# First loads, constants and key masks of a two-layer decoder kernel rearranged

## The chip, the cores and the metric

The kernel runs on one core of one Trainium2 chip. The metric is the device time of one execution in microseconds (us), lower being better. A single profiled execution gives the trace from which all durations below are taken.

## The reference, cut to what matters

Sixteen sequences of 64 tokens, 128 features wide, pass through six blocks, each of the form x = layernorm(x + block(x)): causal self-attention with rotary positions (16 heads of 8), cross-attention to a context with a key mask, a mixture of 8 experts (two per token), wide self-attention (16 heads of 64), a second masked cross-attention, and a feed-forward block with ternary weights. All tensors are float32. What the change touches:

```python
q, k, v = proj(wq, bq), proj(wk, bk), proj(wv, bv)      # first block, biases bq, bk, bv, bp
q, k = _apply_rope(q, cos, sin), _apply_rope(k, cos, sin)
att = softmax(where(causal, q @ k.T / sqrt(8), lowest))
x = layernorm(x + (att @ v) @ wp.T + bp)
scores = where(mask == 0, -1e9, q @ k.T / sqrt(8))       # second block; -1e12 in the fifth
```

The mask is an int32 tensor [16, 1, 1, 64] of zeros and ones. A key counts where it is not zero.

## The kernel before, in words

The 1024 tokens stand as 8 tiles of 128 tokens (two sequences each). All attention and feed-forward tiles before the experts form one software pipeline: 8 tiles of stage `a0` (self-attention, L717 on in the stage class `Narrow`), then 8 of `a1` (cross-attention). In round j of `stream_pe`, `stream_act`, `stream_dve` and `stream_pool` each engine works on up to six tiles at different steps, in an order written out by hand. Tile b (newest) is projected to q and k, tile b-2 is scored and its row maximum taken, tile b-3 is transposed, and so on. Every engine executes its own list in order and waits on semaphores for the others.

One round of `a0` goes: TensorE (PE) projects k and q (L496); ScalarE (ACT) copies both with their bias into TMP (L581); VectorE (DVE) swaps pairs of TMP (L622) and multiplies by the sines (L625) while GpSimd (POOL) multiplies TMP by the cosines (L683, TC) and makes the residual XR = X + bias row (L686); DVE adds to KT and QS (L631, L634); POOL spreads KT into head blocks KB (L671, two of 128x512); PE scores (L524) and adds the causal fill by a bf16 matmul of idb and caus (L529); DVE takes the maximum (L401) and subtracts it (L411); ACT takes the exponential (L417). In `a1` the fill comes from a bf16 matmul of fills and mrb (L531) and the keys are multiplied by mk (L647).

The beginning. SP, the engine that only issues loads, issues in this order: first half of x (tiles 0 to 3), four weights wq, wk, wv, wp (RAWW, inside the tensor U), four biases of the first block (`load_biases(sp, 0)`: bq and bk to qkb, bv to bvc, bp spread over 128 partitions to rowb), second half of x, the context, the gate weights gw, eight later weights, the biases of the second block, the masks (mki is 128 partitions wide, mri six), then the expert weights of four experts and more. ACT issues the identity (part of cst, 64 KB) and then all other constants in one load (537 KB) before it copies anything. The constants' columns are: identity 0 to 127, cosines from 128, sines from 192, head blocks from 256, causal fill from 264, iota from 328, fills from 336, ones from 592, halves from 720, and routing constants up to 1202.

PE starts with `first.pe`: it transposes the first half of x (needs identity and x), then the four weights (needs all four); ACT copies the first group to XT (L281), DVE the second to WT (L283). `first.done(pe)` waits for both copies, and then come the rounds. DVE first waits for identity and all constants, makes idb, caus and fills (L1915 to L1918), then copies WT, then makes onesb, trib and before (L1921 to L1923). POOL waits for all constants, writes the ones columns of VB (L1890), then waits for both halves of x and the four biases. ACT waits for the four biases before its rounds. In round 1 `later` transposes the second half of x, the context and gw, and in rounds 2 and 3 `weights` transposes the later weights. In round 2 DVE runs `masks` (L1769): it compares and subtracts (L1772: 0 or -1), multiplies the result by -1 (L1774), makes mrb (L1775), and waits for its own results. SP waits for the masks before it loads the wide weights over the raw masks in U. Later stages (experts from about 128 us, the wide stage from about 213 us) follow the same rounds.

Of the kernel before, what the change touches and what calls it, by code (L numbers as in the profile page):

```python
# [11 lines left out]
ALU = mybir.AluOpType  # L12
# [3 lines left out]
P = 128  # L16
BATCH, SEQ = 16, 64
# [60 lines left out]
def decoder_kernel(nc, A, out):  # L78
    with ExitStack() as ctx:
# [135 lines left out]


        s_id = sem("identity_loaded")
        s_cst = sem("cst_loaded")
        s_x = [sem("x_loaded_%d" % h) for h in range(2)]
        s_ctx = sem("ctx_loaded")  # L220
# [229 lines left out]
        class Narrow(Stage):  # L450
# [63 lines left out]
            def s_pe(self, pe, job):  # L514
# [11 lines left out]
                for g in range(2):  # L526
                    o = PS[:, B_S + g, :].rearrange("q (h k) -> q h k", h=8)
                    if self.fill is None:
                        m = pe.matmul(o, idb[:, :], bc(caus[:, :], 1, 8), start=False, stop=True)  # L529
                    else:  # L530
                        m = pe.matmul(o, fills[:, self.fill, :], bc(mrb[:, i, :], 1, 8), start=False, stop=True)  # L531
                m.then_inc(self.s_mm.sem, 1)

# [1235 lines left out]
        def masks(dve):  # L1769

            dve.wait_ge(s_m, 16 * 4)
            dve.tensor_scalar(mk[:, :, :], mki[:, :, :], 0.0, 1.0, ALU.is_equal, ALU.subtract).then_inc(s_mk0, 1)  # L1772
            dve.wait_ge(s_mk0, 1)
            dve.tensor_scalar(mk[:, :, :], mk[:, :, :], -1.0, None, ALU.mult).then_inc(s_mk0, 1)  # L1774
            dve.tensor_scalar(mrb[:, :, :], mri[:, :, :], 0.0, None, ALU.is_equal).then_inc(s_mk, 1)  # L1775
            dve.wait_ge(s_mk0, 2)

        def pre_dve(dve, j, late):
            if j == 1 and late:
# [49 lines left out]
        def _(sp):  # L1829
            def load(dst, src, s, **k):  # L1830
                sp.dma_start(dst, src, **k).then_inc(s, 16)

            x = A["x"].rearrange("(t b) s f -> (b s) t f", b=2)
            load(X[:, 0:4, :], x[:, 0:4], s_x[0])
            for n in range(4):
                load(RAWW[:, n, :], A[WNAMES[n]], s_w0)
            load_biases(sp, 0)
            load(X[:, 4:8, :], x[:, 4:8], s_x[1])
            load(CTXR[:, :, :], A["ctx_1024"].rearrange("(t b) s f -> (b s) t f", b=2), s_ctx)
            load(gw[:, :], A["L0_ffn_gate_w"], s_ctx)  # L1840
# [23 lines left out]
            load(routed.rearrange("(p r) f -> p r f", p=P), bc(zero[:, :], 1, ROWS // P), s_zr)  # L1864
            weights.done(sp)
            later.done(sp)
            sp.wait_ge(s_mk0, 2)
            sp.wait_ge(s_mk, 1)
            load(U[:, 0:3 * HEADS * DW], A["L1_attn_W_qkv"], s_wide)
            for e in range(4, EXPERTS):  # L1870
# [29 lines left out]
        @block.scalar  # L1900
        def _(act):
            act.dma_start(ident, table[:, C_ID:C_ID + P]).then_inc(s_id, 16)
            act.dma_start(cst[:, C_ID + P:], table[:, C_ID + P:]).then_inc(s_cst, 16)
            first.copies(act, 0)
            act.wait_ge(s_b[0], 16 * NB)
            stream_act(act, pre, pre_act)
            moe.act(act)
            act.wait_ge(s_fc, 64)
            stream_act(act, post, post_act)

        @block.vector
        def _(dve):
            dve.wait_ge(s_id, 16)
            dve.wait_ge(s_cst, 16)
            dve.tensor_copy(idb[:, :], ident).then_inc(s_bf, 1)  # L1915
            dve.tensor_copy(caus[:, :], cst[:, C_CAUSAL:C_CAUSAL + SEQ]).then_inc(s_bf, 1)
            dve.wait_ge(s_bf, 2)
            dve.tensor_copy(fills[:, :, :], cst[0:6, C_FILL0:C_FILL0 + 2 * P].rearrange("p (l q) -> p l q", l=2))\  # L1918
               .then_inc(s_bfc, 1)
            first.copies(dve, 1)  # L1920
            dve.tensor_copy(onesb[:, :], cst[:, C_ONES:C_ONES + P]).then_inc(s_rt, 1)  # L1921
            dve.tensor_copy(trib[:, :], cst[:, C_BEFORE:C_BEFORE + P]).then_inc(s_rt, 1)
            dve.memset(before[:, 0, :], 0.0).then_inc(s_rt, 1)  # L1923
            stream_dve(dve, pre, pre_dve)
            moe.dve(dve)
            stream_dve(dve, post, post_dve)

        @block.tensor
        def _(pe):
            first.pe(pe)  # L1930
            first.done(pe)
            pe.wait_ge(s_bfc, 1)
            stream_pe(pe, pre, pre_pe)
            moe.pe(pe)
            stream_pe(pe, post, post_pe)
# [17 lines left out]
```

## Time and profile before

| what | us |
|---|---|
| three runs | 394.96, 392.46, 393.14 |
| their median | 393.14 |
| the profiled execution, device time | 389.23 |
| span of its trace (first to last instruction) | 387.4 |
| mean granted TensorE clock in it | 0.949 |

Busy in the profiled execution: PE 341.5 us (88% of the span), weight loads 265.5, DVE 250.6 (65%), POOL 186.1 (48%), ACT 183.7 (47%).

How to read it: the device time of the profiled execution holds 1.8 us outside the span, and it is 3.9 us under the median of the three runs. Times in the rows are microseconds from the first instruction. PE is the matmuls, PEld the weight loads that overlap them, SPq and ACTq the queues' issuing instructions. A clock of 1.00 in a row stands for 2.4 GHz, 0.50 for 1.2 GHz.

### The profile page before, as it was taken

Reading aid. Unit: us, or ns where it says so; the run is one execution under the profiler, and the core shown is the slowest. Engines: PE = TensorE matmul, PEld = TensorE weight load, DVE = VectorE, ACT = ScalarE, POOL = GpSimd, SP = SyncE. Lnnn points to the kernel's source line nnn. Section 1 sums busy time; section 2 is a strip of 40 time slices with the busy share of each in tenths; the row PEclk is TensorE's granted clock in tenths of the full one; section 3 lists DMA queues with packets and bytes.
Section 4 is the critical chain, followed back from the end, with each engine's and each line's share of the span. In section 5 each row is a group of like instructions: output and inputs, shape, how many; then the busy total and the mean of one; then the engine's idle time right before and its main releaser. Section 6 shows DMA issues by size and latency. Waiting matters only on the chain.

```text
span 387.4 us, 9800 instructions
## 1 busy us (share of the span) xinstructions
PE 341.5 (88%) x3718; PEld 265.5 (69%) x3718; DVE 250.6 (65%) x592; ACT 183.7 (47%) x385; POOL 186.1 (48%) x267
## 2 busy tenths in 40 slices
PE   3789899998997089999996798999999999999982
PEld 2556566764897079999995665677777657766662
DVE  1799988888535413573335277845666668886894
ACT  2476567764468423233224243544435356667441
POOL 1867756554454515553313755311212465463673
PEclk9999999999579669999999699999999999999998
DMA  6799930000057111112111110000000000000000
GB/s 195 208 317 254 296 139 2 2 3 2 28 160 217 37 45 48 50 41 56 36 30 34 42 36 15 0 3 2 0 3 3 2 0 3 2 2 3 3 27 27
DMA packets 35938, 22.95 MB, mean 59 GB/s; under 512 B 4142, under 2 KB 33846, under 8 KB 35766
## 3 DMA queue, kind: packets, MB, share of 16 engines
q1 hardware_dynamic: 34582, 19.63, 17.6%
q0 software_dynamic: 1024, 2.10, 1.8%
q8 instruction: 30, 0.49, 0.5%
q10 hardware_dynamic: 288, 0.62, 0.5%
q14 instruction: 14, 0.11, 0.1%
HBM read 14.60 MB, written 7.73 MB: 58 GB/s over the span
## 4 chain that ended last, share of the span: by engine, by line
PE 67%; DVE 12%; issue 7%; POOL 6%; DMA 3%; ACT 2%; SPq 1%; POOLq 0%; DVEq 0%; ACTq 0%
PE banks L427 7%; PE banks L825 7%; PE banks L812 7%; PE banks L547 6%; PE banks L1505 6%; PE banks L1513 6%; PE banks L1536 5%; PE banks L524 4%; PE banks L856 3%; PE banks L1312 2%; PE banks L531 2%; POOL KB L671 2%; PE banks L508 2%; PE banks L371 2%; PE banks L496 2%
## 5 line engine op out<-in xcount | busy, mean ns | idle before, releaser
L671 POOL TENSOR_TENSOR KB<-KT,cst 128x512 f32<-128x512 f32 x48 | 49.3, 1047 | 7.4 <-DVE KT L631 5.6
L331 POOL TENSOR_SCALAR ve<-mv 128x1 f32<-128x1 f32 x40 | 10.6, 266 | 86.3 <-DVE mv L326 86.3
L436 ACT ACTIVATE PT<-banks 128x512 f32<-128x512 f32 x64 | 35.0, 595 | 24.5 <-PE banks L427 23.5
L401 DVE TENSOR_REDUCE mx<-banks 128x16 f32<-128x1024 f32 x32 | 38.6, 1207 | 5.4 <-PE banks L531 4.7
L1528 DVE TENSOR_TENSOR PT<-banks,PR 128x512 f32<-128x512 f32 x23 | 15.9, 691 | 40.4 <-PE banks L1513 35.8
L862 ACT ACTIVATE U<-banks 128x512 f32<-128x512 f32 x40 | 23.9, 597 | 38.0 <-PE banks L825 22.6
L1493 POOL COPY U<-WALL 128x1024 f32 x21 | 21.8, 1040 | 37.7 <-PE banks L1513 36.2
L427 PE MATMUL banks<-cst,PR 128*128 128x128 f32 x256 | 36.6, 288 | 0.5 <-POOL PR L891 0.5
L417 ACT ACTIVATE PR<-PR 128x1024 f32<-128x1024 f32 x32 | 33.8, 1057 | 3.4 <-DVE PR L411 3.2
L812 PE MATMUL banks<-XT,WQKV 128*128 128x128 f32 x256 | 33.3, 293 | 0.4 <-ACT XT L1713 0.4
L812 PEld LDWEIGHTS banks<-XT,WQKV 128*128 128x128 f32 x256 | 31.8, 206 | 1.1 <-ACT XT L1713 0.7
L825 PE MATMUL banks<-WALL,XT 128*64 128x512 f32 x128 | 29.8, 601 | 3.1 <-DVE U L862 2.8
L427 PEld LDWEIGHTS banks<-cst,PR 128*128 128x128 f32 x256 | 29.1, 147 | 4.1 <-issue 2.0
L524 PE MATMUL banks<-KB,QS 64*64 64x512 f32 x192 | 27.6, 614 | 3.1 <-issue 1.5
L411 DVE TENSOR_TENSOR PR<-banks,mx 128x1024 f32<-128x1024 f32 x24 | 29.4, 1224 | 0.8
L547 PE MATMUL banks<-VB,PT 128*64 128x18 f32 x768 | 28.3, 217 | 0.0
L337 DVE TENSOR_SCALAR X<-R,mv,rstd 128x128 f32<-128x128 f32 x40 | 19.2, 479 | 14.1 <-POOL rstd L333 14.1
L547 PEld LDWEIGHTS banks<-VB,PT 128*64 128x64 f32 x768 | 25.9, 145 | 3.2 <-issue 0.8
L862 DVE COPY U<-banks 128x512 f32<-128x512 f32 x24 | 16.2, 686 | 15.0 <-PE banks L825 10.9
L1505 PE MATMUL banks<-XGT,U 128*128 128x128 f32 x184 | 25.7, 285 | 0.0
L1513 PE MATMUL banks<-XGT,U 128*128 128x128 f32 x184 | 25.2, 281 | 0.0
L1536 PE MATMUL banks<-WALL,PT 128*128 x184 | 24.4, 276 | 0.6 <-DVE YS L1544 0.6
(183 smaller groups left out, 700.2 us busy)
## 6 DMA issues: line engine op xcount, KB each, us to landing
routed_rows<-zero SPq DMA_DIRECT2D x1, 4544.0 KB, 20.4
U<-in_L_ffn_wg_dram SPq DMA_DIRECT2D x8, 256.0 KB, 4.5
U<-in_L_ffn_wu_dram SPq DMA_DIRECT2D x8, 256.0 KB, 4.9
U<-in_L_ffn_wd_dram SPq DMA_DIRECT2D x8, 256.0 KB, 5.4
U<-in_L_attn_W_qkv_dram SPq DMA_DIRECT2D x1, 1536.0 KB, 23.0
XG<-routed_rows SPq DMA_DIRECT2D x23, 64.0 KB, 1.8
routed_rows<-YS SPq DMA_DIRECT2D x23, 64.0 KB, 1.6
cst<-shape_constants ACTq DMA_DIRECT2D x1, 537.0 KB, 4.4
```

The source lines that it names most:

```text
L401: dve.tensor_reduce(mx[:, n % 2, :], s, AX.X, ALU.max).then_inc(self.max.sem, 1)
L427: t = pe.transpose(PS[:, B_PT + m, P * (r % 4):P * (r % 4 + 1)], PR[:, n % 2, P * r:P * (r + 1)], ident)
L436: act.activation(PT[:, n % 2, 4 * m:4 * m + 4, :].rearrange("p r q -> p (r q)"), PS[:, B_PT + m, :], ACT.Copy).then_inc(self.pt.sem, 1)
L524: pe.matmul(PS[q, B_S + g, :], QS[f, n % 3, q], KB[f, n % 2, b].rearrange("p h k -> p (h k)"), start=True, stop=False)
L547: m = pe.matmul(PS[64 * b:64 * b + 64, B_Y, w * r:w * (r + 1)], PT[:, n % 2, r, 64 * b:64 * b + 64], VB[:, n % 3, r, b].rearrange("p a e - ...
L671: pool.tensor_tensor(KB[:, n % 2, b], bc(KT[:, n % 2, b, :], 1, 8), bc(cst[:, C_HEAD:C_HEAD + 8], 2, SEQ), ALU.mult).then_inc(self.kb.sem, 1)
L812: m = pe.matmul(PS[:, bank, P * k:P * (k + 1)], WQKV[:, f // 2, P * u:P * (u + 1)], XT[:, P * i:P * (i + 1)], start=True, stop=True)
L825: m = pe.matmul(PS[64 * a:64 * a + 64, bank, :], XT[:, SEQ * (2 * i + b):SEQ * (2 * i + b + 1)], WVO[:, a, 4 * g:4 * g + 4, :].rearrange(" ...
L862: return eng.activation(o, s, ACT.Copy) if part == 0 else eng.tensor_copy(o, s)
L1505: m = pe.matmul(PS[:, j % 2, P * c:P * (c + 1)], WE[:, j % 3, 0, P * c:P * (c + 1)], XGT[:, j % 3, :], start=True, stop=True)
L1513: m = pe.matmul(PS[:, 2 + j % 2, P * c:P * (c + 1)], WE[:, j % 3, 1, P * c:P * (c + 1)], XGT[:, j % 3, :], start=True, stop=True)
L1536: m = pe.matmul(PS[:, 7, 0:P], HT[:, j % 2, c, :], WALL[:, e, 2, P * c:P * (c + 1)], start=(c == 0), stop=(c == CH - 1))
```

## The change

The four biases of the first block are issued by ACT instead of SP. The constants are loaded in three pieces: identity, the 200 columns from cosines to causal fill (semaphore s_cst0), and, after the biases, the rest (874 columns). On SP wq goes ahead of the first half of x, and the second half of x comes right after wp. The key mask is made by one comparison (not equal to zero) instead of a comparison with subtraction and a multiplication. DVE makes idb and caus from what has come, copies WT, and only then waits for the rest of the constants to make fills. PE waits for idb and caus before its rounds, and for fills only at the first score of `a1`.

```diff
--- before.py
+++ after.py
@@ -215,6 +215,7 @@
 
 
         s_id = sem("identity_loaded")
+        s_cst0 = sem("first_constants_loaded")
         s_cst = sem("cst_loaded")
         s_x = [sem("x_loaded_%d" % h) for h in range(2)]
         s_ctx = sem("ctx_loaded")
@@ -528,6 +529,8 @@
                     if self.fill is None:
                         m = pe.matmul(o, idb[:, :], bc(caus[:, :], 1, 8), start=False, stop=True)
                     else:
+                        if i == 0 and self.fill == 0:
+                            pe.wait_ge(s_bfc, 1)
                         m = pe.matmul(o, fills[:, self.fill, :], bc(mrb[:, i, :], 1, 8), start=False, stop=True)
                 m.then_inc(self.s_mm.sem, 1)
 
@@ -1769,11 +1772,9 @@
         def masks(dve):
 
             dve.wait_ge(s_m, 16 * 4)
-            dve.tensor_scalar(mk[:, :, :], mki[:, :, :], 0.0, 1.0, ALU.is_equal, ALU.subtract).then_inc(s_mk0, 1)
+            dve.tensor_scalar(mk[:, :, :], mki[:, :, :], 0.0, None, ALU.not_equal).then_inc(s_mk0, 1)
+            dve.tensor_scalar(mrb[:, :, :], mri[:, :, :], 0.0, None, ALU.is_equal).then_inc(s_mk, 1)
             dve.wait_ge(s_mk0, 1)
-            dve.tensor_scalar(mk[:, :, :], mk[:, :, :], -1.0, None, ALU.mult).then_inc(s_mk0, 1)
-            dve.tensor_scalar(mrb[:, :, :], mri[:, :, :], 0.0, None, ALU.is_equal).then_inc(s_mk, 1)
-            dve.wait_ge(s_mk0, 2)
 
         def pre_dve(dve, j, late):
             if j == 1 and late:
@@ -1831,10 +1832,10 @@
                 sp.dma_start(dst, src, **k).then_inc(s, 16)
 
             x = A["x"].rearrange("(t b) s f -> (b s) t f", b=2)
+            load(RAWW[:, 0, :], A[WNAMES[0]], s_w0)
             load(X[:, 0:4, :], x[:, 0:4], s_x[0])
-            for n in range(4):
+            for n in range(1, 4):
                 load(RAWW[:, n, :], A[WNAMES[n]], s_w0)
-            load_biases(sp, 0)
             load(X[:, 4:8, :], x[:, 4:8], s_x[1])
             load(CTXR[:, :, :], A["ctx_1024"].rearrange("(t b) s f -> (b s) t f", b=2), s_ctx)
             load(gw[:, :], A["L0_ffn_gate_w"], s_ctx)
@@ -1864,7 +1865,7 @@
             load(routed.rearrange("(p r) f -> p r f", p=P), bc(zero[:, :], 1, ROWS // P), s_zr)
             weights.done(sp)
             later.done(sp)
-            sp.wait_ge(s_mk0, 2)
+            sp.wait_ge(s_mk0, 1)
             sp.wait_ge(s_mk, 1)
             load(U[:, 0:3 * HEADS * DW], A["L1_attn_W_qkv"], s_wide)
             for e in range(4, EXPERTS):
@@ -1900,7 +1901,9 @@
         @block.scalar
         def _(act):
             act.dma_start(ident, table[:, C_ID:C_ID + P]).then_inc(s_id, 16)
-            act.dma_start(cst[:, C_ID + P:], table[:, C_ID + P:]).then_inc(s_cst, 16)
+            act.dma_start(cst[:, C_COS:C_IOTA], table[:, C_COS:C_IOTA]).then_inc(s_cst0, 16)
+            load_biases(act, 0)
+            act.dma_start(cst[:, C_IOTA:], table[:, C_IOTA:]).then_inc(s_cst, 16)
             first.copies(act, 0)
             act.wait_ge(s_b[0], 16 * NB)
             stream_act(act, pre, pre_act)
@@ -1911,13 +1914,14 @@
         @block.vector
         def _(dve):
             dve.wait_ge(s_id, 16)
+            dve.tensor_copy(idb[:, :], ident).then_inc(s_bf, 1)
+            dve.wait_ge(s_cst0, 16)
+            dve.tensor_copy(caus[:, :], cst[:, C_CAUSAL:C_CAUSAL + SEQ]).then_inc(s_bf, 1)
+            first.copies(dve, 1)
+            dve.wait_ge(s_bf, 2)
             dve.wait_ge(s_cst, 16)
-            dve.tensor_copy(idb[:, :], ident).then_inc(s_bf, 1)
-            dve.tensor_copy(caus[:, :], cst[:, C_CAUSAL:C_CAUSAL + SEQ]).then_inc(s_bf, 1)
-            dve.wait_ge(s_bf, 2)
             dve.tensor_copy(fills[:, :, :], cst[0:6, C_FILL0:C_FILL0 + 2 * P].rearrange("p (l q) -> p l q", l=2))\
                .then_inc(s_bfc, 1)
-            first.copies(dve, 1)
             dve.tensor_copy(onesb[:, :], cst[:, C_ONES:C_ONES + P]).then_inc(s_rt, 1)
             dve.tensor_copy(trib[:, :], cst[:, C_BEFORE:C_BEFORE + P]).then_inc(s_rt, 1)
             dve.memset(before[:, 0, :], 0.0).then_inc(s_rt, 1)
@@ -1929,7 +1933,7 @@
         def _(pe):
             first.pe(pe)
             first.done(pe)
-            pe.wait_ge(s_bfc, 1)
+            pe.wait_ge(s_bf, 2)
             stream_pe(pe, pre, pre_pe)
             moe.pe(pe)
             stream_pe(pe, post, post_pe)
```

## Rows read from the trace of the kernel before

**Rows 1.** Windows of the whole core: stretch, length, busy and count per engine, granted clock, DMA
```profile
48.00:90.00 42.00, 42.00 (x540) 28.48 (x539) 36.51 (x73) 28.69 (x67) 25.53 (x39) 1.00 0.09 36
```

**Rows 2.** Chain that ended last, 0 to 60 us: start, length, what
```profile
4.64 4.68 DMA rowb<-in_L_attn_bp_dram
...
10.55 0.90 DVE TS L625
```

**Rows 3.** Timeline, 0 to 13 us: start, length, engine, line, what; idle before it
```profile
1.17 0.45 ACTq L1903 DMA_DIRECT2D cst<-shape_constants  x1
...
1.65 1.28 ACT L281 ACT_TABLE_LOAD   x1 [1.65 <-PEq L1943]
...
2.75 0.43 SPq L1831 DMA_DIRECT2D U<-in_L_attn_wp_dram  x1
...
4.24 1.09 PE L270 MATMUL banks<-cst,X 128*128 128x128 f32 x4 [4.24 <-DMA X<-in_x_dram]
...
5.67 0.65 POOL L1890 COPY VB<-cst 128x24 f32<-128x24 f32 x4 [3.93 <-DMA cst<-shape_constants]
...
6.50 1.12 PE L270 MATMUL banks<-cst,U 128*128 128x128 f32 x4 [1.17 <-DMA U<-in_L_attn_wp_dram]
...
7.66 0.69 DVE L283 COPY WT<-banks 128x512 f32<-128x512 f32 x1 [1.20 <-PE banks L270]
...
8.40 0.22 DVE L1922 CAST trib<-cst 128x128 bf16<-128x128 f32 x1
...
8.45 1.19 PE L496 MATMUL banks<-XT,WT 128*128 128x128 f32 x4 [0.83 <-issue]
...
9.35 0.69 ACT L581 ACTIVATE TMP<-banks,qkb 128x128 f32<-128x128 f32 x2 [3.39 <-DMA rowb<-in_L_attn_bp_dram]
...
10.19 1.19 PE L496 MATMUL banks<-XT,WT 128*128 128x128 f32 x4 [0.55 <-ACT TMP L581]
10.44 0.73 POOL L683 TENSOR_TENSOR TC<-TMP,cst 128x256 f32<-128x256 f32 x1 [4.12 <-DMA X<-in_x_dram]
...
10.99 0.79 ACT L581 ACTIVATE TMP<-banks,qkb 128x128 f32<-128x128 f32 x2 [0.95 <-PE banks L496]
```

**Rows 4.** DMA issues of the whole run: median us to landing last
```profile
cst<-shape_constants ACTq DMA_DIRECT2D x1, 537.0 KB, 4.4
...
cst<-shape_constants ACTq DMA_DIRECT2D x1, 64.0 KB, 2.5
```

**Rows 5.** Windows of 2 us: the same columns as rows 1
```profile
4.00:6.00 2.00, 1.09 (x4) 0.72 (x4) 0.29 (x2) 0.60 (x1) 0.33 (x3) 1.00 0.94 278
...
18.00:20.00 2.00, 1.17 (x9) 0.35 (x10) 1.97 (x4) 1.22 (x2) 0.67 (x2) 1.00 0.99 274
```

**Rows 6.** Timeline, 18 to 22 us, DVE and the POOL work that follows
```profile
18.64 0.68 DVE L1772 TENSOR_SCALAR mk<-U 128x1024 f32<-128x1024 int32 x1
...
19.36 0.69 DVE L1774 TENSOR_SCALAR mk<-mk 128x1024 f32<-128x1024 f32 x1
...
19.97 0.41 DVE L1775 TENSOR_SCALAR mrb<-U 6x512 bf16<-6x512 int32 x1
...
20.31 0.42 DVE L622 STREAM_SHUFFLE TS<-TMP 128x256 f32<-128x256 f32 x1
...
21.60 2.04 POOL L671 TENSOR_TENSOR KB<-KT,cst 128x512 f32<-128x512 f32 x2 [2.93 <-DVE KT L631]
```

**Rows 7.** Windows of 5 us where the clock falls and rises: columns as rows 1
```profile
90.00:95.00 5.00, 3.63 (x56) 2.61 (x56) 4.59 (x21) 2.78 (x6) 0.89 (x3) 1.00 0.01 3
95.00:100.00 5.00, 5.00 (x39) 3.60 (x37) 3.60 (x7) 2.57 (x6) 3.34 (x5) 0.50 0.08 28
...
110.00:115.00 5.00, 5.00 (x60) 4.85 (x59) 1.31 (x5) 3.28 (x8) 3.98 (x6) 0.80 0.74 223
```

**Rows 8.** Timeline, 88 to 100 us, PE: the same eight transposes at either clock
```profile
89.95 1.07 PE L427 MATMUL banks<-cst,PR 128*128 128x128 f32 x8
...
96.95 1.97 PE L427 MATMUL banks<-cst,PR 128*128 128x128 f32 x8
```

## The prediction, written before the change was run

> **What bounds the kernel now.** I read the windows of the whole run first, then the chain that ended last, then the timeline of the first 22 us, the DMA issues, and last the windows in which the clock changes. From 48 to 90 us PE is busy for 42.00 of 42.00 us [rows 1]. Before that no engine is full for the whole stretch, and the chain runs from hand to hand, so a cut there can bring PE's full stretch forward as a whole. What follows it is ordered by the same rounds and no load of the beginning is late for it, so a shift of the full stretch should reach the end.
>
> The chain names the row bias (rowb<-bp): issued at 4.64, waited for until 9.32 [rows 2]. A reader would take 3.39 us of ACT waiting for it [rows 3] as the prize. It is not. PE starts the first projections at 8.45 and ACT copies from 9.35, 0.90 later. In round 1, where no load is in the way, PE starts at 10.19 and ACT at 10.99, 0.80 later [rows 3]. The bias is thus late by 0.1 us only. What sets the first copy is the projection, and behind it stands this row of work: PE transposes the weights at 6.50 when wp has landed, DVE copies WT at 7.66, PE projects at 8.45, ACT's two copies end at 10.04, POOL multiplies by the cosines at 10.44 once the second half of x is there, and DVE's product with the sines ends at 11.45 [rows 2, 3]. KT follows and the head blocks after it.
>
> **The change part by part.**
>
> *Loads ahead of the weights.* Up to wp the queues carry 64 (identity) + 537 (constants) + 256 (x) + 4 x 64 (weights) = 1113 KB. At 278 GB/s and a DMA share of 0.94 [rows 5] that is 4.0 us. The weights are there at 6.45, so by this reckoning bytes begin to flow at about 2.4. After the change 64 + 100 (200 columns) + 256 + 256 = 676 KB, and at most 66 KB of biases, stand ahead of wp: 742 KB, 2.7 us, a landing at 5.1. wp's issue stays at 2.75, since x and wq only trade places, and the quickest 64 KB load took 2.5 us [rows 3, 4], so it is not there before 5.25.
>
> *x half a step later.* Its first half is issued one issue (0.5 us) later. Bounds of its landing: 4.24, as now, since 484 KB instead of up to 857 KB go by until it is complete (2.4 + 1.7 = 4.1), and 4.76, if the issue alone sets it. I take 4.3, nearer to the reckoning by bytes. Its transposes take 1.09 [rows 3] and end at 5.4. The weights' transposes then start at 5.4 instead of 6.50: 1.1 us sooner. Bounds: 0 (wp lands as now) and 1.25 (5.25).
>
> *Biases on ACT.* Four issues at the step of SP, (4.64 - 2.75) / 4 = 0.47 us [rows 2, 3], move ACT's table load from 1.65 to about 4.1 and its end to 5.4. The first ACT copy needs x's transposes, which end at 5.4 too, so nothing is lost; even 0.5 us late it would be done before WT is copied at about 7.2. The biases are issued from 1.6 to 3.5. If the row bias again takes 4.68 us, from 3.07, it lands at 7.75, ahead of the first use at 8.15. That pays the 0.1 from above: ACT's copies start at 9.35 - 1.1 - 0.1 = 8.15 and end at 8.95 instead of 10.04.
>
> The trace shows the first loads sharing one stream at a share of 0.94 whether SP or ACT issued them [rows 5]. By the Trainium skill, page "DMA: Bandwidth & Descriptors", section "Issuing engines are not separate DMA queues", loads from SP and ACT use the same DMA engines and interleave, so moving the biases saves issue time only. That speaks against a gain from the move itself; my sum gives it 0.1 us, and by a reading of separate bandwidth it would be no more, since the projection comes later anyway.
>
> *SP's order.* Four issues gone and the second half of x ahead of nothing else new: it and all that follows (context, later weights, masks) is issued 4 x 0.47 = 1.9 us sooner. POOL was released by it at 10.44 [rows 3], which becomes about 8.5, before ACT's copies end at 8.95. So the 0.4 us that POOL lost there go as well. They are hidden in part: DVE's shuffle goes on meanwhile.
>
> *The rest of the constants, later.* This is the risk. 437 KB are issued at about 3.55 instead of at 1.17. With the 4.4 us of the whole [rows 4] they land at 8.0. Other bound: they come last among all up to the context, 1945 KB at 278 GB/s, 2.4 + 7.0 = 9.4. I take 8.1, by the row of the same load. Behind this wait stand POOL's four VB copies (0.65) and DVE's fills and three more small ones (about 0.22 each, 0.9) [rows 3]. POOL is then ready at 8.75 and DVE at 9.0, beside ACT's end at 8.95. I charge 0.05. At the late bound DVE is ready at 10.3, against 10.1 now, and the start loses 0.2 instead of gaining. The early casts of idb and caus move ahead of the WT copy into time in which DVE waits, and cost nothing as the first constants (100 KB, issued at 1.17) need to be there only by about 6.4.
>
> *Sum of the start.* Shuffle at 9.0 (0.45), product with the sines at 9.45. It took 0.90 with POOL at work beside it [rows 2], and will again: end 10.35 against 11.45. Gain 1.1 us, bounds -0.2 and 1.4.
>
> *Masks.* Three operations from 18.64 to the shuffle at 20.31, 1.67 us, with DVE busy 1.97 of 2 us [rows 5, 6]. POOL idles 2.93 us until KT, two steps behind that shuffle [rows 6], and then makes KB. DVE is what comes last here, so its time is the chain's. The multiplication (19.36 to 19.97, 0.61) goes, and the wait between comparison and mrb (0.04) with it: 0.65 us. Bounds: the new comparison reads the same int32 and writes the same float, and lasts 0.68; as short as mrb's 0.41 it would bring 0.27 more; hidden entirely, by PE's scores or by the loads of the masks, the part brings nothing. The masks are issued 1.9 us sooner while DVE comes 1.1 sooner, so the loads give no new wait.
>
> *PE's waits.* PE waits for idb and caus rather than fills: both are made before the WT copy that it waits for anyway. Its new wait for fills stands at the first score of the second stage, some 40 us after they are made. Nothing.
>
> *Total.* 1.1 + 0.65 = 1.75 us. Against its own time the profiled execution would go from 389.23 to 387.5. The three runs have a median 3.9 us above it, so on their footing 393.14 - 1.75 = **391.4 us**. All of it is 0.45%. A measurement of this kernel tells about 1% from no change.
>
> **Rivals.**
>
> *The constants come late* (392.7). The rest of the constants is behind the context, the start gains -0.2, masks 0.65: 0.45 us in all. For it: DVE and POOL both wait for that load, and its issue is 2.4 us later. Against it: it has a queue with nothing else in it.
>
> *The gain is absorbed* (393.1). Where PE becomes full, at 48 us, something else than the chain of the first rounds decides, so that the shift ends there. For it: PE, DVE and POOL are all near their limit in turn. Against it: every operation in between waits for one that shifts too.
>
> *The clock gives more than the change* (383.6). The granted clock is 0.50 from 95 us until 112 (0.80 over 110 to 115 makes the rise at 112.0) after PE had been busy 3.63 of 5 us [rows 7]. Eight transposes take 1.97 at 1.2 GHz and 1.07 at 2.4 GHz [rows 8], so these 17 us hold 17 x (1 - 1.07 / 1.97) = 7.8 us. Is the fall gone in most executions, 391.4 - 7.8 = 383.6. Nothing in the change touches that place but its time.
>
> *An additional low stretch, slower* (399.2). The same price with the other sign: PE works thinly between 18 and 24 us (1.17 of 2 us from 18 to 20 [rows 5]), and starting the first transposes and projections nearer together leaves a like gap in front of round 2. If the clock falls there and holds as long as it did at 95, the loop of scores, maximum and subtraction runs with PE at half speed: 391.4 + 7.8 = 399.2. It decides once a fall is granted before 48 us, where none is now. Against it: such gaps are there already without a fall.
>
> By the Trainium skill, page "TensorE: Matmul & The Clock Gate", section "What's actually happening", the monitor of activity runs freely and is not reset when a kernel starts, so where the clock turns differs between executions. The trace cannot show it with one execution. By that rule both clock cases strike single executions rather than the median, which is why they get little.
>
> **How the numbers follow.** Forecast 0.64, constants late 0.15, absorbed 0.08, clock better 0.08, slower by a low stretch 0.05. The first three all lie within 1%: 0.87. Executions spread by 2.5 us, so 0.05 of them may come out faster by over 1% (below 389.2): faster 0.13, same 0.82, slower 0.05. The forecast's bounds (gain 0.4 to 2.1) with the spread of the runs around them give 387.5 to 394.3; this holds the first three cases and leaves the clock cases out.
>
> **What would show it right or wrong.** PE's transposes of the weights at 5.4 (wrong beyond 6.2); ACT's first copy into TMP at 8.15 after PE and not after a load; POOL's TC near 9.0, and VB's copies done before it (wrong if they wait past 9.0); product with the sines ending at 10.35; one comparison into mk of 0.68 and 1.0 us from its start to the shuffle; the first projection-to-KB rounds of a1 and PE's full stretch beginning 1.7 us sooner. If every mark up to 48 us is 1.7 us sooner but the span isn't shorter, the loss lies in a clock stretch and the windows after 90 us show it.

## The result, and the profile after

The changed kernel takes 395.65 us (median of 6, 395.02 to 396.5), the kernel before on the same chip 392.8 (median of 6): ratio 1.007, 95% interval 1.004 to 1.0101. On another chip two more copies give 1.0046 (0.9989 to 1.0102) and 1.0061 (1.0027 to 1.0094). So it is slower by 0.5 to 0.7%. The prediction was 391.4 with an upper end of 394.3. The profiled execution takes 395.19 us, span 393.2, mean clock 0.949, the same clock as before. "Late" below means later than in the kernel before; "bound" is the end of a range in the prediction.

Timeline of the changed kernel, 0 to 14 us, the lines that answer to [rows 3]:

```profile
1.21 0.42 SPq L1832 DMA_DIRECT2D X<-in_x_dram  x1
...
2.69 0.43 SPq L1832 DMA_DIRECT2D U<-in_L_attn_wp_dram  x1
...
3.59 0.45 ACTq L1906 DMA_DIRECT2D cst<-shape_constants  x1
...
5.19 1.09 PE L271 MATMUL banks<-cst,X 128*128 128x128 f32 x4 [5.19 <-DMA X<-in_x_dram]
...
8.61 1.12 PE L271 MATMUL banks<-cst,U 128*128 128x128 f32 x4 [2.33 <-DMA U<-in_L_attn_wp_dram]
...
10.56 1.19 PE L497 MATMUL banks<-XT,WT 128*128 128x128 f32 x4 [0.83 <-issue]
10.80 1.00 POOL L1891 COPY VB<-cst 128x24 f32<-128x24 f32 x4 [9.07 <-DMA cst<-shape_constants]
...
11.43 0.73 ACT L584 ACTIVATE TMP<-banks,qkb 128x128 f32<-128x128 f32 x2 [4.51 <-PE banks L497]
...
12.19 0.44 DVE L625 STREAM_SHUFFLE TS<-TMP 128x256 f32<-128x256 f32 x1
...
12.32 0.73 POOL L686 TENSOR_TENSOR TC<-TMP,cst 128x256 f32<-128x256 f32 x1 [0.52 <-ACT TMP L584]
...
12.67 0.66 DVE L628 TENSOR_TENSOR TS<-TS,cst 128x256 f32<-128x256 f32 x1
```

Read the brackets. PE waits 2.33 us for wp, which was issued at the forecast moment but lands at about 8.6: the transposes of the weights start at 8.61, not at 5.4, and 2.1 us later than before. ACT's copies wait for the projection (4.51 <-PE), no longer for a bias. POOL's TC follows ACT at once, so the second half of x is in time, but only because ACT is late: it was to be there at about 8.5 and landed at 11.1, 8.0 us after its issue and 0.9 later than before, although it was issued 2.05 us sooner. The issues and landings, answering to [rows 4]:

```profile
X<-in_x_dram SPq DMA_DIRECT2D x2, 256.0 KB, 5.9
cst<-shape_constants ACTq DMA_DIRECT2D x1, 437.0 KB, 7.2
...
U<-in_L_attn_wp_dram SPq DMA_DIRECT2D x1, 64.0 KB, 5.9
rowb<-in_L_attn_bp_dram ACTq DMA_DIRECT2D x1, 64.0 KB, 6.0
```

The chain that ended last now runs through it (start, length, what), where [rows 2] had the row bias:

```profile
2.69 5.88 DMA U<-in_L_attn_wp_dram
8.61 1.12 PE banks L271 x4
```

Where the bytes went is seen in windows of 2 us. The last three columns are clock, DMA share and GB/s. Before:

```profile
2.00:4.00 2.00, 0.00 (x0) 0.00 (x0) 0.00 (x0) 0.93 (x1) 0.00 (x0) 1.00 0.87 286
4.00:6.00 2.00, 1.09 (x4) 0.72 (x4) 0.29 (x2) 0.60 (x1) 0.33 (x3) 1.00 0.94 278
6.00:8.00 2.00, 1.12 (x4) 0.72 (x4) 0.76 (x3) 0.00 (x0) 0.31 (x3) 1.00 0.42 112
8.00:10.00 2.00, 1.19 (x4) 0.93 (x4) 0.63 (x4) 0.65 (x2) 0.00 (x0) 1.00 1.02 303
```

The changed kernel:

```profile
2.00:4.00 2.00, 0.00 (x0) 0.00 (x0) 0.23 (x1) 0.00 (x0) 0.00 (x0) 1.00 0.94 233
4.00:6.00 2.00, 0.81 (x4) 0.72 (x4) 0.20 (x1) 1.28 (x1) 0.00 (x0) 1.00 0.65 140
6.00:8.00 2.00, 0.28 (x2) 0.00 (x0) 0.00 (x0) 0.60 (x1) 0.00 (x0) 1.00 0.53 153
8.00:10.00 2.00, 1.12 (x4) 0.72 (x4) 0.23 (x1) 0.00 (x0) 0.00 (x0) 1.00 1.02 338
```

Both kernels have a stretch of slow flow although much is queued. Before it is seen after 6 us, when the constants are in and wp is about to land (6.5), and little waits for it: ACT's first copy loses at most 0.1 us, POOL's TC 0.4. After the change it covers 4 to 8 us, and wp and the rest of the constants are inside.

The mean flow is not the whole of it. By 5.5 us pieces of about as many bytes had begun on SP's queue as all its loads up to wp hold (512 KB, 0.52 MB), in both kernels (DMA view of 0 to 5.5 us: packets, MB, share; the changed kernel first):

```profile
q1 hardware_dynamic: 1090, 0.52, 32.5%
```

```profile
q1 hardware_dynamic: 1104, 0.50, 31.3%
```

Yet wp landed at 6.5 before and at 8.6 after. Pieces of the second half of x can be among these bytes. So the last of wp's pieces or signals came late while others had moved on; the trace does not say which, nor on which DMA engine.

How does the loss travel? I compared the start of PE's n-th instruction in both traces. The changed kernel is 0.95 us late at x's transposes, 2.11 at the weights', 1.89 from 14 us on. The masks bring it to 1.17, and there it stays up to 90 us. These lines, against [rows 6], show the mask step:

```profile
20.54 0.68 DVE L1775 TENSOR_SCALAR mk<-U 128x1024 f32<-128x1024 int32 x1
...
21.13 0.41 DVE L1776 TENSOR_SCALAR mrb<-U 6x512 bf16<-6x512 int32 x1
...
21.48 0.43 DVE L625 STREAM_SHUFFLE TS<-TMP 128x256 f32<-128x256 f32 x1
```

0.94 us from the comparison to the shuffle instead of 1.67. PE is full in 50 to 92 us (42.00 of 42.00), as in [rows 1]. Behind that the lateness grows to 2.5 us at 120 and to 5.05 at 130. The last step belongs to these copies of expert weights, 1.43 us apart though each lasts 0.60:

```profile
128.09 0.60 ACT L1320 ACTIVATE WALL<-banks 128x512 f32<-128x512 f32 x1 [0.19 <-PE banks L1315]
...
129.52 0.60 ACT L1320 ACTIVATE WALL<-banks 128x512 f32<-128x512 f32 x1 [0.83 <-PE banks L1315]
...
130.95 0.60 ACT L1320 ACTIVATE WALL<-banks 128x512 f32<-128x512 f32 x1 [0.84 <-remote]
```

The same spacing is in the traces of i1, i2 and k2 below, and is missing in f2 and g3, which are the changed kernel itself. All four traces that have it come from chips on which the kernel before takes about 393 us, f2 and g3 from one where it takes 386. So it goes with the execution or the chip and is no part of the change. Its cause stays open, and the 5.7 us between the two profiled spans are not the price of the change: the medians say 2.2 to 2.9.

The clock: over 95 to 112 us [rows 7] the mean is 0.67 here, 0.50 before, and 1.00 in g3, whose clock first falls after 125 us. Executions of one kernel differ in mean clock, on later chips from 0.942 (before: 390.6 us) to 0.964 (385.1 us), so where I write "at equal clock", medians of executions of about equal mean clock are compared (116 of the kernel before; some groups hold only one to three). The ratios mix clocks and are not as sharp.

### The profile page after: what moved, and what is told of

Same layout as the page of the kernel before. It is cut to its first block, busy times and chain, and to the rows that moved or that the text cites. A ratio compares the mean times of both kernels' runs of the same rounds, so it can differ in the third digit from the quotient of the medians.

```text
span 393.2 us, 9800 instructions
## 1 busy us (share of the span) xinstructions
PE 340.8 (87%) x3718; PEld 265.8 (68%) x3718; DVE 249.5 (63%) x591; ACT 184.6 (47%) x385; POOL 187.0 (48%) x267
## 4 chain that ended last, share of the span: by engine, by line
PE 70%; DVE 11%; issue 8%; POOL 4%; DMA 2%; ACT 2%; SPq 1%; another core or an unknown queue 1%; POOLq 0%; DVEq 0%; ACTq 0%
PE banks L428 8%; PE banks L815 6%; PE banks L828 6%; PE banks L1508 6%; PE banks L525 6%; PE banks L550 6%; PE banks L1516 5%; PE banks L1539 5%; PE banks L859 3%; PE banks L497 3%; PE banks L509 2%; PE banks L534 2%; PE banks L372 2%; DMA U<-in_L_attn_wp_dram 1%; PE banks L566 1%
```

## The experiments

Two marks tell most: when the weights' transposes start (wp has landed, and x's transposes are done) and when VB's first copy starts (the rest of the constants has landed). Each kernel has one trace; three traces of the changed kernel have the first mark at 8.26, 8.61 and 8.93, three with the old start at 6.50 to 6.67, so a difference under 0.7 us is weak. The code cuts below are shortened; most leave out the semaphore increments. "PE at 60 us" is the lateness of PE's n-th instruction there against the kernel before on the same chip.

**First set: which part costs.** e1 is before with the masks alone; e2 to e4 put back biases, row or columns to SP behind wp.

```diff
@@ e1: before, masks
-            dve.tensor_scalar(mk[:, :, :], mki[:, :, :], 0.0, 1.0, ALU.is_equal, ALU.subtract).then_inc(s_mk0, 1)
+            dve.tensor_scalar(mk[:, :, :], mki[:, :, :], 0.0, None, ALU.not_equal).then_inc(s_mk0, 1)
-            dve.tensor_scalar(mk[:, :, :], mk[:, :, :], -1.0, None, ALU.mult).then_inc(s_mk0, 1)
@@ e2: changed kernel (e3: the spread row alone; e4: the three columns alone)
-            load_biases(act, 0)
@@ SP, after wp
+            load_biases(sp, 0)
```

> The kernel before with the mask part alone. Both theories agree on the start: all marks up to 18 us as before. Theory (DVE is what comes last in round 2): from round 3 on PE runs 0.65 us ahead of the kernel before, PE's full stretch near 47.3 instead of 48 us, and the time is 0.65 us less, if nothing later gives it back. Rival (the comparison's gain is hidden): nothing moves.

> The changed kernel with the four bias loads back on SP, right behind wp; constants in three pieces, wq ahead of x, masks as changed. Theory (the bias loads, issued before wp's bytes have gone, hold up the engines on which wp waits): wp lands by 5.5 to 6.0 instead of 8.6, the weights' transposes start at 5.9 to 6.3, PE at 48 us is 0.9 to 1.3 us ahead of the kernel before, and the time is 392.8 - 1.1 = 391.7 or a little less. Rival 1 (the second half of x and the context at wp's heels): they stand 1.9 us later here, so this run gives the same, and the next two tell. Rival 2 (the constants in pieces, or wq ahead of x): wp stays at 8 or later. Rival 3, for what is lost behind 90 us: ACT has four instructions less here than in the changed kernel; if its stall at 127 to 131 us hangs on where its instructions lie, it changes or goes.

> The changed kernel with only the spread row bias (128 reads of one row of 512 bytes) back on SP behind wp; the three column loads of 4-byte pieces stay on ACT. If the spread row holds up wp: weights' transposes by 6.3. If the columns do: they still start after 8. If both share it: between 6.5 and 8.

> The changed kernel with only the three column loads (384 pieces of 4 bytes) back on SP behind wp; the spread row stays on ACT. If the columns hold up wp: weights' transposes by 6.3. If the spread row does: still after 8. If it is the second half of x and the context that follow wp more closely than before: this run and the one with the row on SP both stay late, by nearly the same.

| kernel | weights' transposes | VB | ratio (95%) |
|---|---|---|---|
| e1 masks alone | 6.62 | 5.85 | 0.9953 (0.9898 to 1.0009) |
| e2 biases on SP | 6.85 | 6.35 | 1.0043 (1.0001 to 1.0084) |
| e3 row on SP | 8.62 | 10.15 | 1.002 (0.9985 to 1.0054) |
| e4 columns on SP | 8.03 | 7.51 | 1.0009 (0.9962 to 1.0057) |

With the biases back on SP (e2) most of wp's delay is gone, though 6.85 is above the 5.9 to 6.3 expected. With either kind alone on ACT it stays late. What each kind is worth is not separated: the rest of the constants is issued at 3.11 in e3 and 2.14 in e4, against 1.63 in e2, and h1 below shows that its place counts too. In e1 PE comes 0.73 us sooner from the masks on, as forecast. At equal clock e1 and e2 are within 0.3 us of before in most groups.

**Second set: bytes, pieces or addresses.** f1 is before and f2 the changed kernel once more. f3 keeps count and size of every piece but reads other places. It computes with other numbers as the first block's biases. f4 has x first, and the old biases, then the rest of the constants, on SP behind wp.

```diff
@@ f3
-            load_biases(act, 0)
+            for n, src in enumerate(("L0_attn_wq", "L0_attn_wk")):
+                act.dma_start(qkb[:, 0, n:n + 1], A[src][:, 0:1], ...)
+            act.dma_start(bvc[:, 0:1], A["L0_attn_wv"][:, 0:1], ...)
+            act.dma_start(rowb[:, 0, :], A["L0_attn_wp"])
@@ f4, SP after x, wq, wk, wv, wp
+            load_biases(sp, 0)
+            load(cst[:, C_IOTA:], table[:, C_IOTA:], s_cst)
```

> The kernel before, unchanged, for its marks and its clock on the chip on which the next three run. Weights' transposes near 6.5, PE at 48 us as in the first trace within 0.3 us. Executions with the same mean clock agree within 1 us; the spread of the whole comes from the clock stretches behind 93 us.

> The changed kernel, unchanged. Weights' transposes near 8.6, PE 1.0 to 1.4 us behind the kernel before at 48 us, and the same distance between executions of equal mean clock. Theory on the additional 2.5 us that the first trace shows between 125 and 130 us (ACT's copies 1.43 us apart): if it hangs on where ACT's instructions lie, it is there again and executions are 3.5 to 4 us slower than those of before at equal clock; rival: it was that one execution's, and they are 1.2 us slower.

> The changed kernel, whose four bias loads on ACT read as many pieces of the same sizes, but each from a row of its own (columns and rows of weights), so the biases are other numbers. Theory A (many reads of one small place in memory hold up the engines): the weights' transposes start by 6.3. Theory B (the number of small pieces, or four more loads ahead, holds them up): still at 8 or later. The spread row alone (128 pieces of 512 bytes, a size that weights have too) cost 1.2 us at wp, which speaks for A.

> The changed kernel with x first again, the biases on SP behind wp, and the rest of the constants on SP behind the biases, ahead of the second half of x; ACT issues only identity and first constants. Theory (x and the weights wait for whatever shares the engines with them): x lands by 4.0, wp by 5.3, the weights' transposes start by 5.5, WT is copied by 6.6, ACT's first copy is then at 8.3 unless the biases come later, PE at 48 us is 1.4 to 1.9 us ahead of the kernel before. Rival (the reads of the biases then hold up the constants, so that POOL and DVE start late): the first product with the sines ends no sooner than before.

The transposes start at 6.67 in f1, 8.26 in f2, 6.81 in f3 (expected: by 6.3), 5.34 in f4. f3's windows of 2 us, beside those of the changed kernel above, tell why:

```profile
4.00:6.00 2.00, 0.77 (x4) 0.72 (x4) 0.20 (x1) 1.28 (x1) 0.00 (x0) 1.00 0.86 221
6.00:8.00 2.00, 1.44 (x6) 0.72 (x4) 0.04 (x1) 0.60 (x1) 0.00 (x0) 1.00 1.01 338
```

The same number of pieces of the same size no longer slows the flow: 338 GB/s at 6 to 8 us, where the changed kernel has 153, and wp is 1.4 to 2.1 us sooner. What makes the difference is the address: 384 pieces of 4 bytes out of three stretches of 512 bytes, and one stretch of 512 bytes read 128 times. (ACT's queue has 288 packets before and 864 with the biases on it in g1 below: 576 more, 144 for each load, which fits 128 pieces and a few signals each.) In whole time f3 gives 1.0043 (0.998 to 1.0105): too wide to tell, and with other numbers in it. f4 has the earliest weights and still loses (1.0073, 1.0004 to 1.0142), since the slow stretch now holds up what its first rounds need:

```profile
8.97 0.63 ACT L584 ACTIVATE TMP<-banks,qkb 128x128 f32<-128x128 f32 x2 [2.94 <-DMA rowb<-in_L_attn_bp_dram]
...
10.60 1.01 POOL L1893 COPY VB<-cst 128x24 f32<-128x24 f32 x4 [8.86 <-DMA cst<-shape_constants]
```

**Third set: the move alone, and biases without repeated reads.** g1 is before with one edit, the biases on ACT behind the constants. g2 loads the four biases as rows of 512 bytes; PE turns three with the identity and spreads the fourth with a row of ones, and ACT copies them out. It has x first and the rest of the constants on SP behind wp. g3 is the changed kernel a third time. h1 has the rows, but the changed kernel's order.

```diff
@@ g2, h1
-            load_biases(act, 0)
+            for n, b in enumerate("qkv"):
+                act.dma_start(brow[n:n + 1, :], A["L0_attn_b" + b].rearrange("(o p) -> o p", o=1))
+            act.dma_start(bprow[:, :], A["L0_attn_bp"].rearrange("(o p) -> o p", o=1))
@@ PE, after first.pe
+            pe.transpose(PS[:, 4, 0:3], brow[:, :], ident[0:3, 0:3])
+            pe.matmul(PS[:, 4, P:2 * P], ones1[:, :], bprow[:, :], start=True, stop=True)
```

> The kernel before with one edit: the four bias loads are issued by ACT behind the constants (1.6 to 3.5 us) instead of by SP behind wp (3.2 to 5.2). Theory (reads of one small place hold up whatever shares the engines with them): weights' transposes at 7.8 to 8.6 instead of 6.5 to 6.7, PE at 48 us 1.2 to 1.9 us behind. Rival (the harm comes of the biases together with the constants in pieces or wq ahead of x): it stays within 0.4 us of the kernel before at either mark.

> The changed kernel without the many reads of one place: the four biases of the first block come as four rows of 512 bytes, each one piece, on ACT; PE turns three of them into columns and spreads the fourth with a row of ones, ACT copies the results (three small copies more, two PE operations more). x first again, the rest of the constants on SP behind wp. Theory: no stretch of 100 GB/s between 4.5 and 7.5 us, wp lands by 5.3, weights' transposes by 5.5, the rest of the constants by 8, ACT's first copy into TMP at 8.3 to 8.6, PE at 48 us 1.3 to 2.0 us ahead of the kernel before, and about as much less time at equal clock. Rival (bandwidth sets these landings and the places read do not matter): wp by 5.3 too, but the constants land after 9.5 and the start gains nothing.

> The changed kernel once more, for executions that can be set beside those of before at equal clock, and for ACT's copies between 125 and 132 us. Theory (the 2.5 us there were one execution's): not there, and 1.2 to 2.2 us slower than before at equal clock. Rival (they come and go with the execution): there in this profile, with executions 3 us or more slower at equal clock.

> The changed kernel in its own order of loads (wq ahead of x, the rest of the constants on ACT), with the one edit that the four biases come as four rows of one piece each and PE turns them. It tells how much of the gain of the kernel with rows, x first and the rest on SP is the rows' alone. Theory (x is late in the changed order because the large pieces of the constants share the engines with it, and this costs little once the biases hold up nothing): x lands between 4.8 and 5.7, the weights' transposes follow at 5.9 to 6.8, PE at 48 us is 0.5 to 1.3 us ahead of the kernel before, at least 0.5 us less far than with x first. Rival (the order of loads is worth nothing beside the rows): PE at 48 us as far ahead as there, 1.9 us or more.

g1, timeline:

```profile
9.46 1.12 PE L270 MATMUL banks<-cst,U 128*128 128x128 f32 x4 [3.93 <-DMA U<-in_L_attn_wp_dram]
```

More than the 7.8 to 8.6 expected, PE is 2.5 us late at 60 us, and the ratio is 1.0052 (1.0022 to 1.0081). The move alone, with nothing else changed, delays PE more than the whole change does (g3: 8.93 and 1.14 us late; f2: 1.58 us late), though its time is not longer (g3 1.0061, f2 1.0046). g2, timeline:

```profile
4.38 1.09 PE L277 MATMUL banks<-cst,X 128*128 128x128 f32 x4 [4.38 <-DMA X<-in_x_dram]
...
5.46 1.11 PE L277 MATMUL banks<-cst,U 128*128 128x128 f32 x4
...
7.65 1.01 POOL L1899 COPY VB<-cst 128x24 f32<-128x24 f32 x4 [5.79 <-DMA cst<-shape_constants]
...
8.28 0.73 ACT L590 ACTIVATE TMP<-banks,qkb 128x128 f32<-128x128 f32 x2 [0.43 <-PE banks L503]
```

These are the forecast's own marks: 5.4, 8.15, ready before 9.0. Its flow at 4 to 8 us is 276 and 310 GB/s. But h1 missed: 7.71 where 5.9 to 6.8 was expected, PE 0.8 us late at 60 us where 0.5 to 1.3 ahead was expected, ratio 1.0042 (1.0016 to 1.0067). It has no repeated read in it:

```profile
4.00:6.00 2.00, 0.87 (x4) 0.71 (x4) 0.20 (x1) 0.87 (x1) 0.00 (x0) 1.00 0.72 191
6.00:8.00 2.00, 0.51 (x4) 0.29 (x3) 0.00 (x0) 0.60 (x1) 0.00 (x0) 1.00 1.06 331
```

So the repeated reads are not the only cause.

**Fourth set: what else delays wp.** In i1 and i2 ACT issues the rest of the constants only when the weights have landed, in h1 and in the changed kernel.

```diff
+            act.wait_ge(s_w0, 16 * 4)
             act.dma_start(cst[:, C_IOTA:], table[:, C_IOTA:]).then_inc(s_cst, 16)
```

```diff
@@ j2 (from g2), k2 (from before); j1 is the reverse in the changed kernel
+            load(RAWW[:, 0, :], A[WNAMES[0]], s_w0)
             load(X[:, 0:4, :], x[:, 0:4], s_x[0])
-            for n in range(4):
+            for n in range(1, 4):
```

j1 is the changed kernel with x ahead of wq again, j2 is g2 with wq ahead of x, j3 is g2 again, k2 is before with wq ahead of x and nothing else.

> The kernel of h1 (biases as four one-row loads, order of the changed kernel) with one wait more: ACT issues the rest of the constants only when the four weights have landed. Neither the reads of one small place nor the rest of the constants stand beside wp. Theory (the repeated reads and the rest of the constants each delay wp): the weights' transposes start at 5.3 to 6.0, against 7.71 in h1. Rival (in h1 the four row loads or the order of x and wq delay wp): 7.4 or later. The rest then lands at about 9 to 10, so VB and fills are later than in h1, and the whole gains at most 1 us over h1; its whole says little, the mark of the transposes says all.

> The changed kernel with one wait more: ACT issues the rest of the constants only when the four weights have landed, so that the biases' repeated reads alone stand beside wp. Theory (the repeated reads alone are enough): the weights' transposes start at 7.5 to 8.9, about as in the changed kernel (8.26 to 8.93). Rival (the rest of the constants is what delays wp, the biases only by its side): 5.5 to 6.5. The rest lands later than in the changed kernel, by 3 us or more, so the whole is no faster than the changed kernel and 0 to 2 us slower than it at equal mean clock.

> The changed kernel with one part undone: the first half of x is issued ahead of wq again. x should land at 4.2 to 4.5 instead of 4.9 to 5.2. Theory (hot reads and the rest of the constants delay wp whatever the order of x and wq; the order alone moves x): the weights' transposes at 7.9 to 8.9 as in the changed kernel. Rival (the order is a third cause): 7.5 or earlier, as wp lands about 1 us sooner with x out of the way. At equal mean clock the time is as the changed kernel's within 0.5 us by the theory, 0.7 to 1.2 us shorter by the rival.

> The kernel of g2 (biases as rows, rest of the constants on SP behind wp) with one difference: wq is issued ahead of the first half of x, as in the changed kernel. If the order is a third cause, as 6.52 in i1 against 5.46 in g2 suggests, the weights' transposes start at 6.2 to 6.7 and x lands at 4.9 to 5.2. If 6.52 in i1 came from another chip or from its wait, they start at 5.4 to 5.8.

> The kernel of g2 once more, on the chip of j1 and j2: the control for both, and whether the best version's gain is there on another chip. Weights' transposes at 5.3 to 5.6; 1 to 2 us shorter than the kernel before at equal mean clock. If the chip is what moved i1, they start later than 5.9 here too.

> The kernel before with the order of wq and the first half of x alone changed. x should be issued 0.46 us later and land at 4.9 to 5.4 instead of 4.5. If the order alone moves wp, as 6.36 against 5.65 in the kernels with rows suggests, the weights' transposes start at 7.2 to 7.8 instead of 6.67, and the kernel is 0.4 to 1.1 us slower at equal mean clock. If the order matters only where the biases' repeated reads are ahead of wp (here they are behind it), the transposes start at 6.5 to 7.0 and the time is that of before within 0.3 us.

Start of the weights' transposes:

| beside wp | wq first | x first |
|---|---|---|
| repeated reads and rest | 8.26 to 8.93 (the change) | 6.03 (j1) |
| repeated reads, all constants in one load ahead of them | not tried | 9.46 (g1) |
| repeated reads | 7.63 (i2) | not tried |
| rest of constants | 7.71 (h1), 6.81 (f3), 6.85 (e2) | not tried |
| all constants in one load | 7.05 (k2) | 6.50 to 6.67 (before, e1, f1) |
| neither | 6.52 (i1; 5.3 to 6.0 expected), 6.36 (j2) | 5.46 (g2), 5.65 (j3), 5.34 (f4) |

The repeated reads cost 1.1 us in a pair on one chip (i2 against i1). The rest of the constants costs 1.2 us in h1 against i1, on different chips, but only 0.3 in f3 and e2. The time at which it is issued may decide: at 1.63 in e2, 3.15 in h1 and 3.59 in f3; that was not tested. In j2 the same load is issued at 3.18, as in h1, but on SP's queue behind wp, and wp is not held up. The order takes 0.7 to 0.9 us in j2 against j3 and g2, and 2.2 to 2.9 in j1 against the change. It is no cure by itself: g1 has x first and the latest wp of all. So three things delay wp here, and their delays don't add up. j1 was the surprise; the theory had 7.9 to 8.9. Its windows show what the order decides:

```profile
4.00:6.00 2.00, 1.08 (x4) 0.71 (x4) 0.20 (x1) 1.85 (x2) 0.00 (x0) 1.00 0.83 119
6.00:8.00 2.00, 1.14 (x5) 0.77 (x5) 0.69 (x1) 0.03 (x1) 0.00 (x0) 1.00 0.96 189
```

The slow stretch is all there, 119 GB/s at 4 to 6 us; wp slipped through ahead of its worst part, and the rest of the constants did not:

```profile
11.13 1.00 POOL L1891 COPY VB<-cst 128x24 f32<-128x24 f32 x4 [9.39 <-DMA cst<-shape_constants]
11.17 0.32 DVE L1923 CAST fills<-cst 6x256 bf16<-6x256 f32 x1 [3.29 <-DMA cst<-shape_constants]
...
11.70 0.42 DVE L625 STREAM_SHUFFLE TS<-TMP 128x256 f32<-128x256 f32 x1
```

ACT has TMP's first copies done at 9.6, and DVE comes to them at 11.70, held by the fills. PE is 1.6 us late at 60 us, more than in g3, with the weights 2.9 us sooner. f2 is as late, 1.58. So j1 is as slow as the change: 1.0131 (1.0027 to 1.0235) from 4 executions, three of them of low clock, and these give 393.42 against 390.6 us at equal clock. k2: in the kernel before the order alone moves x from 4.51 to 6.17 and the weights from 6.67 to 7.05:

```profile
6.17 1.09 PE L270 MATMUL banks<-cst,X 128*128 128x128 f32 x4 [6.17 <-DMA X<-in_x_dram]
```

PE is 0.5 us late at 60 us, the time the same (1.0012, 0.9978 to 1.0047). By its expectation the transposes should have been at 7.2 or later if the order alone moved wp, at 7.0 or sooner if not. 7.05 lies between, but the landing decides it (last number: us from the issue, at 2.69 in k2):

```profile
U<-in_L_attn_wp_dram SPq DMA_DIRECT2D x1, 64.0 KB, 4.0
```

wp is there at 6.7, as in f1 (issued 2.75, 3.9 us); its transposes only wait for x's on PE. So here the order does not move wp; x is late by far more than the 0.46 us of its issue.

i1 and i2 lose at the whole (1.0089 and 1.0145): the rest lands so late that their fills start at 11.42 and 13.21, and ACT, held by the new wait, loads its table only at 6.89 and 7.97. The mark was what they were for.

**The fastest version.** g2 and j3 are one kernel on two chips: 385.02 and 384.74 us; ratios to the kernel before 0.998 (0.9946 to 1.0015) and 0.9963 (0.9945 to 0.9982). The first is not clear of no change, the second is; at equal clock most groups of both are 1.1 to 1.4 us shorter. With wq first (j2) it gives 1.0023 (0.998 to 1.0065).

## Why the prediction was wrong

*Loads ahead of the weights.* This step failed. It counted 742 KB at 278 GB/s and put wp at 5.1 to 5.25; wp landed at 8.6. "At most 66 KB of biases" were counted as ordinary bytes, while with them beside the other loads the flow is 140 and 153 GB/s at 4 to 8 us. The sum also took the mean for the last piece: SP's queue had begun 0.52 MB by 5.5 us, nearly as reckoned, and wp's last piece or signal came 3 us behind. The trace of before had the warning: 112 GB/s with a DMA share of 0.42 at 6 to 8 us, just when SP's biases ran, and 4.68 us for a row of 64 KB. I read that as a late bias and not as a flow that everyone shares. I took the bound "0 (wp lands as now)" for the worst; it was 2.1 us above it.

*x half a step later.* Also failed: 4.3 was taken, 4.76 was the bound, 5.19 came. j1 brings it to 4.31 and k2 shows it in the kernel before. Its transposes ended at 6.3, so this alone took 0.9 of the forecast gain.

*The rest of the constants, later.* 8.1 taken, 9.4 the bound, 10.8 measured. Same cause. In the first trace it was not charged in the end, because the weights were later still: DVE waited 0.76 us for TMP, not for constants. In f2, the same kernel, it was: fills wait until 11.96 and the shuffle starts at 12.49, 0.7 us after TMP. In j1 it is what decides.

*Biases on ACT.* Four issues of 0.45 to 0.48 and a table load ending at 5.35: right, and hidden. The 0.1 us that it was to win was hardly there: ACT copies 0.87 us behind PE now, 0.90 before. That the move costs nothing else was wrong; g1 has it at 2.8 us for the transposes. The rule of the Trainium skill, page "DMA: Bandwidth & Descriptors", section "Issuing engines are not separate DMA queues", fits what g1 shows: ACT's bias loads hold up SP's wp. From its words that starting loads on several engines only saves issue time I took that a move does no harm, which it does not say; where all loads share the same engines, the move put slow pieces beside urgent ones. The same page, section "Queues, rings and completion order", says that a load's signal is written only after all earlier writes of the same DMA engine, from any queue. By this rule wp's signal would stand behind bias pieces begun before it. The late wp fits, the 0.52 MB begun by 5.5 us too; no run here separates late data from a late signal.

*SP's order, PE's waits.* PE's waits were right: it waits for neither idb nor fills. The second half of x was issued as forecast but landed at 11.1, not 8.5; TC did not wait for it only because ACT was late too.

*Masks.* 0.65 us forecast, 1.89 to 1.17 = 0.72 measured in the profiled pair, 0.73 in e1.

*A shift reaches the end.* Only roughly. From 55 to 90 us it stays within 0.1 us. At equal clock e1's 0.73 us arrive as 0.2 or nothing (0.4 in one execution), g1's 2.5 late as 0.8 to 3.0, g3's and f2's 1.14 and 1.58 late as 1.7 to 2.5 (3.6 in one). Profiles of equal mean clock agree better: against f1, g1's 2.5 arrive as 2.3 to 2.4 and e1's 1.1 us of lead at 60 us as 0.6 to 0.7. What between 95 and 145 us adds or takes up to about 1 us stays open. So of the 2.2 to 2.9 us that the change costs, 1.1 to 1.6 are shown to arise in the first rounds; the rest is not explained.

*Rivals.* "The constants come late" was half true, with its price on the wrong step. My argument against it, that the load "has a queue with nothing else in it", was wrong by the change itself: the four bias loads stand ahead of it on ACT's queue. "An additional low stretch" is out: the mean clock is the same. The rival missing was the simplest: what is moved to ACT delays what it was moved away from.

## What to carry to other kernels

Moving a load to another queue does not take it out of the way of the first one; ask which loads will be in flight beside it and whether someone waits for them. Before you sum bytes at a rate, look in the windows for stretches where the DMA engines carry little although loads are queued, and find what runs there: a column with 4 bytes per partition or a row spread over 128 partitions is small in bytes and here held up every load beside it. Load such vectors as one row, let an idle TensorE turn or spread them, and put the largest late load behind the urgent small ones on their own queue, not beside them on another (6.36 in j2 against 7.71 in h1, on two chips).

## What the hardware showed that was not expected

- Many reads of one small place slow all queues: about 100 GB/s between 5 and 7 us instead of the 270 to 360 of f3, which has the same count and sizes. With three columns of 128 pieces alone or one row read 128 times alone on ACT wp is still late (8.62 and 8.03), but there the rest of the constants is issued later too.
- The mean flow does not tell when wp lands: in the changed kernel SP's queue had begun 0.52 MB by 5.5 us, as much as stands up to wp, and wp landed at 8.6 (before: 0.50 MB and 6.5).
- A load of 437 KB in large pieces on ACT's queue came with wp landing 1.2 us later (h1 against i1), with 191 GB/s at 4 to 6 us and 331 after; issued 0.44 us later, in f3, only 0.3.
- A 64 KB load issued 0.46 us ahead of x's 256 KB made x land 0.5 to 1.7 us later (j2 against j3: 4.80 and 4.27; k2 against f1: 6.17 and 4.51). In k2 wp landed as before. Bytes alone don't explain that; the cause is open.
- A bias of one row takes ACT 0.24 to 0.27 us to issue (the first 0.63), a spread or column load 0.45 to 0.48.
